# Moving the gathers of a fused decoder layer's attention: two back to back behind slots 1 and 9, in place of one each in slots 2, 6, 10 and 14

## The reference

```python
x = _layernorm(x + _L0_attn_ref(x, A, B, W, b))            # u = x B^T; h_t = A h_(t-1) + u_t; h W^T + b
x = _layernorm(x + _L0_xattn_ref(x, ctx, ctx, Wq, ...))    # 16 heads of 16, rotary, |i - j| <= 50, softmax
x = _layernorm(x + _L0_ffn_ref(x, router_w1, ..., w3))     # 16 experts, 64 tokens of each batch by top-k
```

## Time and profile before

| | us |
|---|---|
| median of 3 runs | 1072.51 (1072.12 to 1072.58) |
| the profiled execution | 1072.09 |
| its span, first to last instruction | 1070.3 |
| PE busy | 991.9 (93%) |
| DVE busy | 729.6 (68%) |
| ACT busy | 591.3 (55%) |
| POOL busy | 672.7 (63%) |

### The profile page before, as it was taken

The page is one execution under the profiler, slowest core; times in us unless marked ns, Lnnn a source line. Parts: engine busy times, 40 slices in busy tenths (PEclk is TensorE's granted clock), DMA queues, the critical chain, the costliest instruction groups (busy, mean ns, idle before and its releaser), DMA issues.

```text
span 1070.3 us, 21269 instructions
## 1 busy us (share of the span) xinstructions
PE 991.9 (93%) x6436; PEld 845.4 (79%) x6436; DVE 729.6 (68%) x2168; ACT 591.3 (55%) x1234; POOL 672.7 (63%) x784
## 2 busy tenths in 40 slices
PE   4799999999989998879999999999999999999990
PEld 3578778777877877658898888888888888888880
DVE  4678888888877798757554787565556756765633
ACT  1155565556565555456656555555555556555642
POOL 5556666666666565267757665776666767666543
PEclk8899999999999999899999999999999999999995
DMA  6344344433333332525676666666676666666636
GB/s 191 84 103 98 100 106 103 103 99 102 102 101 97 85 81 70 182 94 168 156 223 124 160 141 168 136 158 152 160 218 158 141 155 149 147 155 143 184 54 176
DMA packets 114918, 142.56 MB, mean 133 GB/s; under 512 B 15104, under 2 KB 88064, under 8 KB 114688
## 3 DMA queue, kind: packets, MB, share of 16 engines
q1 hardware_dynamic: 86432, 105.56, 34.2%
q0 software_dynamic: 24576, 33.57, 18.1%
q10 hardware_dynamic: 3808, 2.22, 0.7%
HBM read 90.70 MB, written 29.36 MB: 112 GB/s over the span
## 4 chain that ended last, share of the span: by engine, by line
PE 52%; ACT 1%; DMA 1%; POOL 1%; issue 1%; DVE 0%; ACTq 0%; POOLq 0%; SPq 0%
PE gate_bank L1349 16%; PE attn L1349 16%; PE value_bank L1349 16%; PE turn_bank L1359 2%; DMA last<-acc_rows 0%; ACT last L1590 0%; DMA acc_rows<-y,slots_now 0%; PE attn L1432 0%; PE attn L1406 0%; POOL acc_rows L1294 0%; DVE stats L1627 0%; DVE hidden L1620 0%; ACTq L1594 0%; ACT w_hi L1482 0%; POOL rstd L167 0%
## 5 line engine op out<-in xcount | busy, mean ns | idle before, releaser
L1294 POOL DMA_INDIRECT acc_rows<-y,slots_now x128 | 205.6, 1607 | 137.4 <-issue 73.4
L787 ACT ACTIVATE probsT<-scoreT 128x356 f32<-128x356 f32 x256 | 117.7, 468 | 137.6 <-PE scoreT L618 113.3
L945 DVE CUSTOM_DVE_ANT_0 scored<-score,band 128x178 f32<-128x178 f32 x512 | 149.9, 337 | 63.3 <-PE score L589 59.4
L1620 DVE TENSOR_TENSOR hidden<-gate,value_bank 128x512 f32<-128x512 f32 x128 | 87.9, 687 | 152.7 <-ACT gate L1495 152.6
L1495 ACT ACTIVATE gate<-gate_bank 128x512 f32<-128x512 f32 x128 | 76.6, 598 | 188.3 <-PE value_bank L1349 188.3
L1349 PE MATMUL attn<-w_hi,h_hi 128*128 128x256 f32 x512 | 146.1, 285 | 0.2
L1349 PE MATMUL attn<-w_hi,h_lo 128*128 128x256 f32 x512 | 143.3, 280 | 0.0
L1349 PE MATMUL attn<-w_lo,h_hi 128*128 128x256 f32 x512 | 143.3, 280 | 0.0
L589 PE MATMUL score<-k_stack,q_stack 96*128 96x178 f32 x512 | 123.8, 325 | 7.2 <-DVE nmax L945 4.2
L589 PEld LDWEIGHTS score<-k_stack,q_stack 96*128 96x128 f32 x512 | 88.9, 194 | 37.1 <-DVE nmax L945 17.3
L618 PE MATMUL scoreT<-q_stack,k_stack 97*128 97x356 f32 x256 | 116.5, 456 | 0.0
(11 more groups left out here) (214 smaller groups left out, 2374.9 us busy)
## 6 DMA issues: line engine op xcount, KB each, us to landing
arena<-in_w SPq DMA_DIRECT2D x96, 512.0 KB, 4.0
k_stack<-high_k SPq DMA_DIRECT2D x128, 64.0 KB, 2.2
q_stack<-high_q SPq DMA_DIRECT2D x128, 64.0 KB, 2.3
arena<-in_xT SPq DMA_DIRECT2D x16, 256.0 KB, 2.9
arena<-in_x SPq DMA_DIRECT2D x16, 256.0 KB, 3.1
arena<-in_cT SPq DMA_DIRECT2D x16, 256.0 KB, 3.7
k_stack<-low_k SPq DMA_DIRECT2D x64, 64.0 KB, 2.3
q_stack<-low_q SPq DMA_DIRECT2D x64, 64.0 KB, 2.2
```

The lines of the kernel that those rows point to most:

```text
L787: nc.scalar.activation(probsT[g % 2][:, u % HG, :, :].rearrange("p a s -> p (a s)"), scoreT[u % 2][:, 0:2 * SPAN], ACT.Exp, scale=1.0 / DH ...
L945: op = nc.vector.tensor_tensor_reduce(scored[t % 2][:, q, :], score[t % 2][:, q * SPAN:(q + 1) * SPAN], band[:, q, :], -1.0, BIG, ALU.add, ...
L1294: nc.gpsimd.indirect_dma_start(dram["acc"][c], bass.IndirectOffsetOnAxis(ap=now[:, m:m + 1], axis=0), y[m][:], None, compute_op=ALU.add).t ...
L1620: nc.vector.tensor_tensor(hidden[f % 2][:], gate[f % 2][:], value_bank[f % 2][:], ALU.mult).then_inc(hidden_ready, 1)
```

## The change

The gathers of a pair, even group and odd group, stand back to back behind `turned_heads` of slot 1 (pair -2) and of slot 9 (pair -1). `gather` takes the group in place of the slot. In slot 1 they stand ahead of the product K. `keep_values` moves on ACT from slots 7 and 15 to slots 10 and 2; its place inside the slot is the same, behind the exponential and, in slot 2, behind `biased(it, 0)`. DVE's odd sums stay in slots 3 and 11; only the way in which their pair is named changes. All waits are those of before.

```diff
+        GATHERED = {1: (-4, -3), 9: (-2, -1)}
...
-            def gather(it, t):
-
-                g = group(t, 14)
+            def gather(it, g):
+
                 if has(it, g):
...
-                    if t in (2, 6, 10, 14):
-                        gather(it, t)
+                    if t in (1, 9):
+                        for g in GATHERED[t]:
+                            gather(it, g)
...
             def keep_values(it, t):
 
-                g = group(t, 15)
+                g = GATHERED[t - 1][0]
...
-                    if t in (7, 15):
+                    if t in (2, 10):
                         keep_values(it, t)
...
-                    if t in (3, 11) and has(it, group(t, 15)) and not only(it, NB, t, 11):
-
-                        p = group(t, 15) // 2
+                    if t in (3, 11) and has(it, -1) and not only(it, NB, t, 11):
+
+                        p = -1 if t == 11 else -2
```

## The result

| | before | after |
|---|---|---|
| median us | 1072.55 | 1108.78 (1101.47 to 1111.88, 4 runs) |
| ratio, 95% interval | | 1.0327 [1.0272, 1.0381] |
| the profiled execution | 1072.09 | 1101.47 |
| its span | 1070.3 | 1099.7 |

The change is slower, as forecast, but by 36 us in the medians where 18 were forecast and 24.5 were the far end of the range. The profiled execution was the shortest of the four of the changed kernel: 29.4 us over the one before. The trace explains these 29.4; of the 7 us between it and the median there is no trace, only TensorE's mean granted clock of each run: 0.974 in the profiled one, 0.967, 0.965 and 0.961 in the three longer ones.

A forecast was written before the change was run, and what follows sets the result against it. The prediction took a loop through DVE, not busy PE, to set the batch period; batch losses of 9.6, 1.5, 2.4, 1.1, 3.9 and 0.5 and -0.8 for the drain made 18.2 us: 1072.5 + 18 = 1090.5 us, own range 1086 to 1095, 8-in-10 range 1080 to 1097.

The forecast's parts named there:

- The second gather at 0.62: PE, slots 1 and 9: the second gather of a pair costs 0.62 us, 0.31 less than a lone one.
- the first rival: Whole kernel: PE is the bound and the saved mode switches count, 32 x 0.31 = 10 us faster, 1062.5; chance 0.05.
- Slot 1 later by 1.45: PE, slot 1: two gathers ahead of the keys' product make everything behind them 1.45 us later.
- keep_values holds the odd sums, 1.60 late: DVE, slot 3: the odd sums wait for ACT's keep_values, starting 1.60 us late, against 0.5 by PE alone.
- The rival of a short wait: Only PE's shift reaches DVE: 0.5 - 0.3 - 0.1, some 0.2 us per batch, about 1076.5; chance 0.09.
- No second wait in slots 9 and 10: ACT's keep_values of slot 10 ends about 1 us before DVE asks for it, so no second wait.
- The gap of 0.27 is eaten, x2cur 1.3 late: DVE behind the odd sums: its one gap absorbs some lateness, so x2cur and maxima 12 to 15 are 1.3 us late.
- 0.09 of slack, period 27.3: Batch end: scores of the next slot 0 have 0.09 us slack, so the period grows by 1.2 to 27.3 us.
- Batches 2 to 9 are alike: 8 x 1.2: Each of batches 2 to 9 grows by the same 1.2 us, 9.6 together.
- Batch 10 at 2.4, batch 11 at 1.1: Batch 10 loses about 2.4 us, keep_values standing behind table loads and silu; batch 11, with an added product, 1.1.
- Batches 1 and 12 to 14: Batch 1 loses 1.5 us by the same chain; batches 12 to 14, with routing on DVE, 3 x 1.3 = 3.9.
- Batch 15 and the ends: Batch 15, without keys ahead of keep_values, loses 0.5 us; the drain changes by -0.8, between -1.4 and +0.6.

The follow-up runs named there:

- e4: The changed kernel with keep_values moved to slots 1 and 9 on ACT and 33 increments ahead of PE's first step: 1083.18 us, ratio 1.0115.
- e9: The changed kernel with 33 increments on PE, and on DVE in slot 3 the keys' rotation ahead of the odd sums: 1085.44 us, ratio 1.0142.
- e2: The kernel before with 223 increments ahead of PE's first product, bringing its loop to the changed kernel's position within blocks of 256: 1113.06 us, ratio 1.0381.
- e7: The kernel before with the loops of all five engines written out: 1070.71 us, ratio 0.9991.
- e1: The changed kernel with 33 semaphore increments ahead of PE's first step: 1101.15 us, ratio 1.0290.
- e5: The changed kernel with only PE's loop over batches 2 to 9 written out, no instruction added: 1100.07 us, ratio 1.0272.
- e3: The changed kernel with keep_values in slots 1 and 9 instead of 2 and 10 on ACT: 1093.85 us, ratio 1.0188.
- e12: The changed kernel with 160 increments ahead of PE's first step: 1122.40 us (one run).

## Why the prediction was wrong in size and right in kind

By its own steps:

- *The second gather at 0.62*: right, 0.60 against 0.93 for a lone one. The Trainium skill (TensorEngine Tiling (Array Packing), Key Properties) says that a change of tiling mode drains the engine; the runs agree with it as far as 0.3 us for each pair. That it would be time saved was the first rival, and it fell: PE was never the bound.
- *Slot 1 later by 1.45*: right. DVE's wait for slot 2's scores went from 1.74 to 3.27 us, 1.53 more.
- *keep_values holds the odd sums, 1.60 late*: right, 1.68; by PE alone it would have been 0.60 (e4), for 0.5. e9 and e4 take away the wait in two ways and get the same 1.1 us back. The rival of a short wait fell (its own sum, 0.5 - 0.3 - 0.1, is 0.1 for each batch and not 0.2).
- *No second wait in slots 9 and 10*: right, mixed waits for ACT once in each batch; the margin, "about 1 us", is 0.6 by the forecast's own terms (290.6 - 290.0).
- *The gap of 0.27 is eaten, x2cur 1.3 late*: right, 1.34.
- *0.09 of slack, period 27.3*: there was no slack. The 0.09 was read where batch 9 ends, behind which PE's code is straight. Inside the loop PE starts 0.24 behind the end of the read of head 14's maximum, from batch 2 to 8 in the kernel before and in the kernel after (0.27 once, and batch 5 left out), so all of x2cur's lateness counts: in batch 8 it comes 21.78 behind slot 1's scoreT for 20.43, 1.35 later, and slots 0 and 1 add 0.06. The period was 27.48, +1.41 for +1.2, and in batches 3 and 7, where x2cur is 1.5 late, up to +1.6. Over batches 2 to 9 this is 2.1 us.
- *"Batches 2 to 9 are alike: 8 x 1.2"*: this is the step that failed. Each row of a kernel before says what an operation costs there; none says where the code lies. Batch 5 lost 5.9 us to a jump into code no longer held, and batch 6 1.3 more than its share to the other engines' jumps, which before had hidden in all but 0.6. Neither was among the rivals.
- *Batch 10 at 2.4, batch 11 at 1.1*: the place was right and the size half: 4.6 and 2.4. The odd sums were late as computed (3.92 of waiting), but the stop was followed by 10 us at half clock, and the forecast had priced a fall of the clock only for the batches 13 to 15. e4, with keep_values ahead of the silu, gives 30.10 and 30.17. Some of the 4.6 is luck of the kernel before, which kept its clock there (28.41) where e2 and e7 did not (29.25 and 29.24).
- *Batches 1 and 12 to 14*: 2.0 and 4.9 for 1.5 and 3.9, the regular miss again. *Batch 15 and the ends*: 3.0 us better than forecast, 1.0 of that in batch 15, 1.3 ahead of batch 1 and 0.7 behind batch 15. The 1.3 is luck: in the seven profiled kernels without increments batch 1 starts anywhere between 60.2 and 65.0 us.

The misses add up: +0.5 (batch 1), +9.3 (2 to 9), +2.2, +1.3, +1.0 (12 to 14), -1.0 (15) and -2.0 (the ends) are 11.3, from the forecast 18.2 to the measured 29.4, rounded. Without the hole (e1, e5) the kernel is still 2.7 to 2.9% slower, beyond the range, so the hole alone does not explain the miss: it is 5.9 of the 11.3, and the rest is batch 6, batches 10 and 11 with their half clock and a period that was set 0.2 to 0.4 short.

Open: why three of four runs of the changed kernel were 5 to 10 us longer than the one with a trace (their lower mean clock fits more stretches at half clock, but no trace shows where); why e1 gained so little as a whole; why the clock fell in batch 2 of e5; the shares of DVE, ACT, POOL and SP in batch 6.

## What to carry to other kernels

A change that only reorders instructions can still move a loop in its engine's code, and in the new position the jump back can have to fetch: look at the last and the first operation around a loop's branch for idle time by "issue", and test with a few harmless instructions ahead of the loop, or with the loop written out. When a wait is added on the engine that paces a batch, its price is the time in which that engine stands still, and moving one independent operation ahead of it gets it back as well as making the awaited thing earlier. Before you call a short distance between two rows slack, look at the same two rows in other batches: one that is the same in each is a wait and gives nothing away.

## What the runs showed of the hardware

- TensorE's loop body of 1729 recorded instructions ran its second trip without fetching: in the kernel before no packet of PE's instruction queue started between 178.6 and 296.8 us, and the branch took 238 ns. In a bad position (e2 has the very same body) the branch took 3.6 to 4.1 us (after, e2, e3, e12) and fetching went on through the whole second trip, 9 to 10 packets more of 16 KB. The Trainium skill (Runtime: NRT & Kernel Launch, Instruction fetch mechanics) says that a taken branch to code outside the held window has to fetch it before it goes on; the traces agree, with those times. It gives TensorE's instruction memory as 2048 instructions, refilled in blocks of 256, with which a loop of 1729 that stayed held agrees; in its notes it also speaks of a window of two blocks, from which this loop differs, and there the measurement decides.
- Crossing from block to block in straight code cost nothing that can be seen: e7, all loops written out, is 0.9991 [0.9976, 1.0006] of the kernel before.
- Increments of an unused semaphore are not free where nothing hides them: batch 1 started at 65.8 us with 60 of them on PE and at 81.0 with 160, which is 0.15 us for each of the last hundred, and 223 in the kernel before moved it from 61.5 to 92.4. For 33 and 60 the delay can't be told from the spread of the kernels without increments, 60.2 to 65.0.
- The same wait is longer inside PE's loop than in straight code: the scores of slot 0 start 0.24 us behind the end of the read of head 14's maximum in the loop of the kernel before, and 0.06 behind it in e7, which has the same order of instructions written out. What in the loop makes the difference was not tested.
- A stop of PE can be paid twice. Around the silu the kernel before stood still for 2.68 us and kept the granted clock at 1.00 (2.4 GHz) from 313 to 325 us; the kernel after stood still for 2.19 us there and then ran at 0.50 (1.2 GHz) from 340 to 350, standing still for another 0.22 and 0.77 us in that stretch. e4, with a stop of 2.92 us there, has a mean of 0.83 from 320 to 330. e2 and e7 stood still for the same 2.68 us as the kernel before and fell to 0.50 for 3.4 us (e2 from 357.7 to 361.1). So the length of the stop alone doesn't decide it, and what else does the runs don't show.
